# Windowed attention over two layers: position bias and mask move from eight TensorE passes per strip to eight VectorE additions

## The chip, the core and the metric

The kernel runs on one core of a Trainium2 chip. The metric is the device time of one execution in microseconds. The core has TensorE (PE in the rows: matrix passes, whose weight loads are listed apart as PEld), VectorE (DVE), ScalarE (ACT) and GpSimd (POOL), each with an instruction queue of its own, and SyncE (SP), whose queue issues all transfers here. Matrix results go into one of eight banks of PSUM; the other tiles lie in SBUF. Engines wait for each other by semaphores that count finished work.

## The reference

Two Swin layers run one after the other on `x` of 32 x 56 x 56 x 96, layer 0 with 4 heads and layer 1 with 12. In outline, for one layer:

```
h    = roll(LN(x), -3, -3), cut into windows of 7 x 7 = 49 tokens
q, k, v = h @ qkv_w + qkv_b
attn = (q * scale) @ k.T + rel_bias[head] + mask[window]      # 49 x 49, float32
o    = softmax(attn) @ v @ proj_w + proj_b
x    = x + roll(unwindow(o), 3, 3)
x    = x + fc2( [LN3, layer 0 only] gelu(LN(x) @ fc1_w + fc1_b) )
```

`rel_bias` depends on head, query and key. `mask` is 0 or -100 and differs from 0 only in the last row and the last column of windows. The term `rel_bias + mask` is what the change is about.

## The kernel before

The work is cut into 256 strips (`ns`), each a row of eight windows of one image. The eight windows lie as `PAIRS` = 4 pairs, so a strip is 4 x 98 = 392 tokens and most tiles are some 98 to 128 partitions by 392 columns. The scores of a strip stand in units of 113 x 392: the first window of each pair on partitions 0 to 48, the second on 64 to 112, and 8 blocks of 49 keys beside each other. Layer 0 has two units (`sc00`, `sc01`), layer 1 six (`sc10` to `sc15`); each has a PSUM bank while it lives.

All engines run the same loop over `i` (`iterate`), and in body `i` they work on strips of different age: `Strip(i, 2)`, called `s2`, is the strip that was loaded two bodies before. `LAST` is the largest age, so there are 256 + `LAST` bodies; those at the start and the end leave out the stages whose strip doesn't exist. The order within a body is written out by hand for each engine in its own `body(i)`. `BANKS` lists the uses of the seven shared banks (use, age, bank) in the order of TensorE's body, and `bank_free` makes a matrix pass wait until the use before it in that bank was read. The eighth bank, `ps_o`, holds the attention output.

The stages of a strip for one layer, by helper:

- `stats` (DVE), `inverse_root` and `norm` (POOL), `xT` (PE) and `turned` (ACT) normalise and transpose the tokens: tile `xnA` ahead of attention, `xnM` ahead of the MLP.
- `q`, `k`, `v` (PE) with `q_out`, `k_out`, `v_out` (ACT). `variants` and `spread_v` (SP) then rearrange keys and values by DMA into `kM` and `vM`.
- `scores` (PE). For each unit one pass `tleft` x `table` (L462, 104 rows, 113 x 392 out, start=True) writes bias and mask into the bank. Then the products of queries and keys (L471, start=False) are added to it: 24 instructions in the rows for three units of layer 1, 32 for both of layer 0.
- `shift` (DVE). The maximum over the keys, negated, is read from the bank (L826), then scores plus `negmax` go to `shifted` in SBUF (L830). That frees the bank.
- `exps` (ACT, L662), `probs_turn` (PE, L483, transpose into a `T` bank), `probsT_out` (ACT, L669), `attend` (PE, L503, into `ps_o`), `normalise` (DVE), `o_turn` (PE), `o_out` (ACT), `project` (PE), `residual` (DVE).
- `fc1` (PE, L539 to L542: three passes, of which the last needs `low_part`, a DVE subtraction, L817), `gelu` (ACT), `fc2` (PE, L559 and L565), and to finish: for layer 0 `squares` (POOL), `third_stats`, `finish0`; for layer 1 `finish1` (DVE, L861), which writes `y_out`.

Ahead of the loop the constants are loaded (L303), and DVE splits the table into a high and a low part (L786, L787).

Of the kernel before, what the change touches and what calls it, by code (L numbers as in the profile page):

```python
# [26 lines left out]
NREG = 6  # L27
BK = 2 * TOK + NREG
# [14 lines left out]
def shape_constants():  # L43
# [3 lines left out]

    left = np.zeros((BK, SP), np.float32)
    for part in (0, 1):
        for h in HALF:  # L50
            left[part * TOK + np.arange(TOK), h + np.arange(TOK)] = 1
    for q in range(TOK):
        left[2 * TOK + rr[q], HALF[0] + q] = 1
        left[2 * TOK + 2 + 2 * rr[q] + rc[q], HALF[1] + q] = 1
    k["tleft"] = left


    right = []
# [36 lines left out]
def swin_program(nc, d, out, ns=NSTRIP, last_row_from=NSTRIP - NSTRIP // ROWS_IN_IMAGE):  # L95
# [3 lines left out]
    with ctx:  # L99
# [13 lines left out]
        def rows_of(ap, step, n, *dims):  # L113
# [4 lines left out]
        tleft_in = sb("tleft_in", [BK, SP])  # L118
        tlow = sb("tlow", [BK, 1])
# [61 lines left out]
        t_in = [t[0:BK, :, :].rearrange("p u k -> p (u k)") for t in (shifted, probs)]  # L181
# [29 lines left out]
        s_s = pairsem("s_s")  # L211
        s_mx = pairsem("s_mx")
# [18 lines left out]
        BANKS = [("o1", 3, 7), ("T01", 1, 2), ("f1_1_1", 4, 5), ("xtA0", 0, 0), ("o0", 1, 7), ("oT1", 3, 1),  # L231
# [839 lines left out]
```

## Time and profile before

| | |
|---|---|
| median of 3 runs | 7130.31 us (7128.76 to 7131.41) |
| the profiled execution | 7130.83 us, its span 7129.1 us, mean granted TensorE clock 0.997 |
| instructions in the span | 284978 |
| HBM | 17 GB/s over the span; the DMA engines are 17.5% busy |

The profiled execution is within 0.6 us of the median; 1.7 us of it lie outside the span. The busy digits of all engines stay level from the second to the last but one of the 40 slices, so nearly the whole time is one repeated strip, and the fill and the drain of the pipeline are small. A busy share counts an instruction from its start to its end. TensorE and VectorE instructions overlap at their ends, so the distance from one start to the next is what one of them costs in a row of its kind.

### The profile page before, as it was taken

Reading aid. Unit: us, or ns where it says so; the run is one execution under the profiler, and the core shown is the slowest. Engines: PE = TensorE matmul, PEld = TensorE weight load, DVE = VectorE, ACT = ScalarE, POOL = GpSimd, SP = SyncE. Lnnn points to the kernel's source line nnn. Section 1 sums busy time; section 2 is a strip of 40 time slices with the busy share of each in tenths; the row PEclk is TensorE's granted clock in tenths of the full one; section 3 lists DMA queues with packets and bytes.
Section 4 is the critical chain, followed back from the end, with each engine's and each line's share of the span. In section 5 each row is a group of like instructions: output and inputs, shape, how many; then the busy total and the mean of one; then the engine's idle time right before and its main releaser. Section 6 shows DMA issues by size and latency. Waiting matters only on the chain.

```text
span 7129.1 us, 284978 instructions
## 1 busy us (share of the span) xinstructions
PE 6951.3 (98%) x98848; PEld 5895.1 (83%) x98848; DVE 5031.9 (71%) x18727; ACT 4674.0 (66%) x9220; POOL 4523.6 (63%) x4612
## 2 busy tenths in 40 slices
PE   6999999999999999999999999999999999999999
PEld 5888888888888888888888888888888888888887
DVE  5777777777777777777777777777777777777775
ACT  3666666666666666666666666666666666666665
POOL 3666666666666666666666666666666666666665
PEclk9999999999999999999999999999999999999999
DMA  1111111111111111111111111111111111111111
GB/s 49 47 46 46 46 46 45 46 45 46 45 46 45 46 45 46 45 47 45 47 45 47 45 47 45 47 44 47 44 48 44 48 44 48 43 48 43 48 43 37
DMA packets 604563, 325.43 MB, mean 46 GB/s; under 512 B 450142, under 2 KB 604128, under 8 KB 604320
## 3 DMA queue, kind: packets, MB, share of 16 engines
q1 hardware_dynamic: 604528, 324.96, 17.5%
q8 instruction: 22, 0.36, 0.0%
q14 instruction: 13, 0.11, 0.0%
HBM read 80.71 MB, written 38.54 MB: 17 GB/s over the span
## 4 chain that ended last, share of the span: by engine, by line
POOL 30%; PE 27%; issue 24%; DVE 17%; POOLq 1%; DVEq 0%; SPq 0%; DMA 0%; ACT 0%
POOL hid_sq L956 8%; POOL x_biased L947 7%; PE ps L422 5%; PE ps L526 5%; PE ps L430 5%; POOL hid_ss L958 4%; POOL rstd L967 4%; POOL rstdM L928 4%; PE ps_o L503 3%; PE ps L515 3%; POOL rstdA L928 3%; DVE x_next L890 3%; DVE bnA L801 2%; DVE bnM L801 2%; DVE o_norm L841 2%
## 5 line engine op out<-in xcount | busy, mean ns | idle before, releaser
L928 POOL TENSOR_TENSOR rstdM<-var_epsM,minus_half 98x4 f32<-98x4 f32 x512 | 515.4, 1007 | 1292.6 <-DVE var_epsM L809 1292.6
L830 DVE TENSOR_TENSOR shifted<-ps,negmax 113x392 f32<-113x392 f32 x2048 | 1161.4, 567 | 213.2
L669 ACT ACTIVATE probsT<-ps 98x392 f32<-98x392 f32 x2048 | 952.3, 491 | 431.3 <-PE ps L483 419.7
L928 POOL TENSOR_TENSOR rstdA<-var_epsA,minus_half 98x4 f32<-98x4 f32 x512 | 518.0, 1012 | 1100.0 <-DVE var_epsA L809 1100.0
L826 DVE TENSOR_REDUCE negmax<-ps 113x8 f32<-113x392 f32 x2048 | 1142.7, 558 | 56.4 <-PE ps L471 28.1
L686 ACT ACTIVATE hid<-ps,bfc 128x392 f32<-128x392 f32 x1536 | 873.0, 587 | 416.3 <-PE ps L542 399.2
L662 ACT ACTIVATE probs<-shifted 113x392 f32<-113x392 f32 x2048 | 997.7, 526 | 23.5 <-DVE shifted L830 15.2
L483 PE MATMUL ps<-ident,probs 113*98 113x113 f32 x8192 | 990.7, 264 | 9.2 <-ACT probs L662 7.7
L503 PEld LDWEIGHTS ps_o<-vM,probsT 98*49 98x49 f32 x32768 | 793.8, 125 | 195.6 <-DVE o_norm L841 128.2
L503 PE MATMUL ps_o<-vM,probsT 98*49 98x50 f32 (+1 forms) x32768 | 851.4, 201 | 78.9 <-DVE o_norm L841 78.7
L483 PEld LDWEIGHTS ps<-ident,probs 113*98 113x98 f32 x8192 | 800.9, 129 | 52.8 <-ACT probs L662 9.6
L653 ACT ACTIVATE vA<-ps 98x400 f32<-98x400 f32 (+1 forms) x512 | 260.5, 509 | 754.9 <-PE ps L440 754.9
L471 PE MATMUL ps<-kM,qT 48*49 48x98 f32 (+1 forms) x20480 | 687.2, 299 | 0.0
L559 PE MATMUL ps<-wfc,hid 128*98 128x97 f32 x6144 | 662.8, 254 | 0.0
L539 PE MATMUL ps<-xnT_high,wfc_high 96*128 96x392 f32 x1536 | 613.8, 400 | 1.2 <-ACT xnT_high L632 1.2
L559 PEld LDWEIGHTS ps<-wfc,hid 128*98 128x98 f32 x6144 | 596.7, 167 | 0.2
L956 POOL TENSOR_TENSOR hid_sq<-hid 128x1176 f32<-128x1176 f32 x256 | 549.7, 2147 | 59.8 <-ACT hid L686 59.8
L471 PEld LDWEIGHTS ps<-kM,qT 48*49 48x49 f32 (+1 forms) x20480 | 430.4, 118 | 188.4 <-issue 172.4
L559 PE MATMUL ps<-par,hid 128*98 128x96 f32 x6144 | 577.9, 251 | 0.7 <-ACT hid L686 0.7
L852 DVE TENSOR_TENSOR x_mid<-x_again,ps 98x384 f32<-98x384 f32 x256 | 141.8, 554 | 605.6 <-PE ps L526 605.6
L677 ACT ACTIVATE oT<-ps 96x392 f32<-96x392 f32 x512 | 252.4, 493 | 472.5 <-PE ps L515 472.5
L559 PEld LDWEIGHTS ps<-par,hid 128*98 128x98 f32 x6144 | 556.7, 168 | 1.2 <-ACT hid L686 1.2
(99 smaller groups left out, 15077.7 us busy)
## 6 DMA issues: line engine op xcount, KB each, us to landing
kM<-kT SPq DMA_DIRECT2D x512, 85.8 KB
vM<-vA SPq DMA_DIRECT2D x1024, 41.3 KB
vM<-vA SPq DMA_DIRECT2D x1024, 38.3 KB
x_in<-in_x SPq DMA_DIRECT2D x256, 147.0 KB
x_again<-in_x SPq DMA_DIRECT2D x256, 147.0 KB
kM<-kT SPq DMA_DIRECT2D x1024, 36.8 KB
x_keep<-x_next SPq DMA_DIRECT2D x256, 147.0 KB
out_y<-y_out SPq DMA_DIRECT2D x256, 147.0 KB
```

Of the source, the lines that this page charges most:

```text
L471: mm = pe.matmul(ps[bank_of[f"sc{L}{u}"]][HALF[h]:HALF[h] + TOK, n * p:n * (p + 1)], qT[L][r, t:t + TOK], kM[L][r, :, t:t + TOK], start=Fa ...
L483: mm = pe.transpose(ps[bank_of[f"T{L}{u}"]][0:PT, n * SP:(n + 1) * SP], probs[:, unit_buffer(L, u), n * PT:(n + 1) * PT], ident[0:SP, 0:SP])
L503: mm = pe.matmul(ps_o[HALF[h]:HALF[h] + TOK, col:col + width], probsT[:, unit_buffer(L, u), p * heads // 2 + n, h, :], vM[L][:, 2 * (first ...
L539: pe.matmul(g[:, 0:ST], wfc1_high[L][:, w], xnT_high[L][:, :], start=True, stop=False)
L559: mm = pe.matmul(g[0:PT, p * step:p * step + width], hid[L][:, c, t], w, start=(c == 0), stop=(c == HCH - 1))
L662: act.activation(probs[:, buf, :], shifted[:, buf, :], ACT.Exp).then_inc(s_ex[L], 1)
L669: act.activation(probsT[:, unit_buffer(L, u), :, :, :], free(ps[bank_of[f"T{L}{u}"]][0:PT, 0:1], (SP, 4), (64, 2), (1, TOK)), ACT.Copy).th ...
L686: act.activation(hid[L][:, c, :], ps[bank_of[f"f1_{c}_{L}"]][:, 0:ST], ACT.Gelu, bias=bfc1[L][:, c:c + 1])\
L826: dve.tensor_reduce(negmax[:, buf, :], s, AX.X, ALU.max, negate=True).then_inc(s_mx[L], 1)
L830: dve.tensor_tensor(shifted[:, buf, :].rearrange("p (h k) -> p h k", k=TOK), s, free(negmax[:, buf, 0:1], (1, 8), (0, TOK)), ALU.add).then ...
L928: pool.tensor_tensor(rstd[n][:, :], var_eps[n][:, :], minus_half[:, :], ALU.pow).then_inc(s_rstd[n], 1)
L956: pool.tensor_tensor(hid_sq[:, :, :], hid[0][:, :, :], hid[0][:, :, :], ALU.mult).then_inc(s_sq, 1)
```

## The change

The table passes L462 go. The first product of queries and keys in each piece of a bank now has start=True and overwrites it. A new helper `bias` on DVE adds the table to the bank in place, 113 x 392 in float32, and counts `s_sb`, for which `shift` now waits; `shift` itself is as before. The table is kept as float32 on 113 partitions (mask loaded from a host array, then two additions ahead of the loop) instead of as a split pair on 104. DVE also clears seven banks ahead of the loop. `scores` waits for queries, keys and banks first and then issues its products. For layer 0 there is one new pass of 1 x 1 ahead of them.

The written-out orders of all five queues are new, as are the banks, and `LAST` is 5 instead of 4: attention of layer 0 is now finished at age 1 and 2, layer 1 starts at age 3.

```diff
-LAST = 4
+LAST = 5
@@ constants
-        t_high = sb("t_high", [BK, NT], f32r)
-        tleft = sb("tleft", [BK, SP], f32r)
-        table = sb("table", [BK, 2 * NT], f32r)
+        table = sb("table", [SP, 2 * NT])
@@ loads
-        loads = [(ident[:, :], d["ident"]), (tleft_in[:, :], d["tleft"]), (tlow[:, :], d["tlow"])]
-        for v in (0, 1):
-            loads += [(t_in[v][0:2 * TOK, :], d["tab"]), (t_in[v][2 * TOK:BK, :], d["tmask"][:, v * NT:(v + 1) * NT])]
+        loads = [(ident[:, :], d["ident"]), (t_in, d["tab"]), (table[:, :], d["mask"])]
@@ scores
-                for u in units:
-                    if free_from := bank_free(x, f"sc{L}{u}"):
-                        pe.wait_ge(*free_from)
-                    if u == units[-1]:
-                        pe.wait_ge(s_qe[L], x.count(1, 1))
-                        pe.wait_ge(s_km[L], x.count(16 * VARIANTS[L], 16 * VARIANTS[L]))
-                    pe.matmul(ps[bank_of[f"sc{L}{u}"]][0:SP, 0:UNIT_COLS], tleft[:, :], table_of(x, L, u),
-                              start=True, stop=False, skip_group_check=True)
+                pe.wait_ge(s_qe[L], x.count(1, 1))
+                pe.wait_ge(s_km[L], x.count(16 * VARIANTS[L], 16 * VARIANTS[L]))
+                for free_from in banks_free(x, [f"sc{L}{u}" for u in units]):
+                    pe.wait_ge(*free_from)
+                if L == 0:
+
+                    pe.matmul(ps[bank_of["sc00"]][0:1, 0:1], ident[:, 0:1], ident[:, 0:1], start=True, stop=True, skip_group_check=True)
...
-                                           kM[L][r, :, t:t + TOK], start=False, stop=True, skip_group_check=True)
+                                           kM[L][r, :, t:t + TOK], start=True, stop=True, skip_group_check=True)
@@ DVE, ahead of the loop
+            for bank in ps[:7]:
+                dve.memset(bank[:, :], 0.0).then_inc(s_memset, 1)
...
-            dve.tensor_copy(tleft[:, :], tleft_in[:, :])
             for v in (0, 1):
                 half = slice(v * NT, (v + 1) * NT)
-                done(dve.tensor_copy(t_high[:, :], t_in[v]))
-                done(dve.scalar_tensor_tensor(out=table[:, half], in0=t_high[:, :].bitcast(f32), scalar=tlow[:, 0:1],
-                                              in1=t_in[v], op0=ALU.mult, op1=ALU.add))
+                done(dve.tensor_tensor(table[:, half], table[:, half], t_in, ALU.add))
@@ DVE, in the loop
+            def bias(x, L, u):
+
+                if x.exists(ns):
+                    dve.wait_ge(s_s[L], x.count(UNITS[L], u + 1))
+                    s = ps[bank_of[f"sc{L}{u}"]][0:SP, 0:UNIT_COLS]
+                    dve.tensor_tensor(s, s, table_of(x, L, u), ALU.add).then_inc(s_sb[L], 1)
+
             def shift(x, L, u):
                 if not x.exists(ns):
                     return
-                dve.wait_ge(s_s[L], x.count(UNITS[L], u + 1))
+                dve.wait_ge(s_sb[L], x.count(UNITS[L], u + 1))
@@ TensorE's body: the first lines, and the last
+                o_turn(s2, 0)
+                xT(s3, "A1")
+                o_turn(s4, 1)
+                project(s2, 0)
+                k(s3, 1)
+                fc1(s5, 1, 0)
+                project(s4, 1)
...
+                xT(s2, "M0")
+                scores(s3, 1, (0, 1, 2))
...
                 attend(s1, 0, 0)
                 attend(s1, 0, 1)
+                scores(s0, 0, (0, 1))
+                xT(s4, "M1")
```

How TensorE's queue moves. Before, from the transpose of `xnM` (layer 0, age 1) to the first `fc1` of layer 0:

```order
L414 MATMUL ps<-ident,xnM 96x98 x4
L462 ISA
L462 MATMUL ps<-table,tleft 113x392
L462 ISA
L462 MATMUL ps<-table,tleft 113x392
L461 REGISTER_ALU
L462 ISA
L462 MATMUL ps<-table,tleft 113x392
L471 MATMUL ps<-kM,qT 49x196 x12
L539 MATMUL ps<-xnT_high,wfc_high 128x392
```

The same place now, from `xnM` of layer 0 (age 2) on, the line numbers being those of the changed kernel (L459 scores, L471 turn of probabilities, L527 fc1):

```order
L411 MATMUL ps<-ident,xnM 96x98 x4
L446 ISA
L459 MATMUL ps<-kM,qT 49x196 x12
L469 REGISTER_ALU
L471 MATMUL ps<-ident,probs 98x113 x4
L527 MATMUL ps<-xnT_high,wfc_high 128x392
```

The three table passes are gone, and a turn of probabilities of layer 0 stands between the scores and `fc1`.

TensorE's later queue now, between the second turn of layer 1's probabilities and the end of its attention:

```order
L471 MATMUL ps<-ident,probs 98x113 x4
L469 REGISTER_ALU
L471 MATMUL ps<-ident,probs 98x113 x4
L491 MATMUL ps_o<-vM,probsT 49x18 x24
L469 REGISTER_ALU
L471 MATMUL ps<-ident,probs 98x113 x8
L467 REGISTER_ALU
L471 MATMUL ps<-ident,probs 98x113 x4
L491 MATMUL ps_o<-vM,probsT 49x18 x24
```

Before, all six `attend` calls of layer 1 (48 rows of 49x18) stood together at the top of the body. Now they are in two halves, in the body in which the scores were made.

VectorE's queue before, from `low_part` of layer 0 into the shifts of layer 1:

```order
L817 TENSOR_TENSOR xnT_low<-ps,xnT_high 96x392
L823 REGISTER_ALU
L826 TENSOR_REDUCE negmax<-ps 113x8
L828 REGISTER_ALU
L830 TENSOR_TENSOR shifted<-ps,negmax 113x392
L823 REGISTER_ALU
L826 TENSOR_REDUCE negmax<-ps 113x8
L828 REGISTER_ALU
L830 TENSOR_TENSOR shifted<-ps,negmax 113x392
```

The same place now (L812 low_part, L820 bias, L828 and L832 shift):

```order
L812 TENSOR_TENSOR xnT_low<-ps,xnT_high 96x392
L818 ISA
L820 ISA
L820 TENSOR_TENSOR ps<-ps,table 113x392
L818 REGISTER_ALU
L820 ISA
L820 TENSOR_TENSOR ps<-ps,table 113x392
L818 REGISTER_ALU
L820 ISA
L820 TENSOR_TENSOR ps<-ps,table 113x392
L828 TENSOR_REDUCE negmax<-ps 113x8
```

Three additions now stand between `low_part` and the first shift. Behind the three shifts come `finish1`, two more additions, two shifts, one addition, `third_stats` and the last shift.

## Rows read from the trace of the kernel before

**Rows 1.** The page, busy time of each engine (share of span):
```profile
PE 6951.3 (98%) x98848; PEld 5895.1 (83%) x98848; DVE 5031.9 (71%) x18727; ACT 4674.0 (66%) x9220; POOL 4523.6 (63%) x4612
```

**Rows 2.** Groups by line, TensorE and ScalarE: busy us, mean ns, idle before:
```profile
L503 PE MATMUL ps_o<-vM,probsT 98*49 98x50 f32 (+1 forms) x32768 | 851.4, 201 | 78.9 <-DVE o_norm L841 78.7
L462 PE MATMUL ps<-table,tleft 104*113 (+1 forms) x2048 | 531.5, 361 | 4.0 <-DMA kM<-kT 2.2 <-DVE shifted L830 1.3 <-DVE y_out L861 0.5
L662 ACT ACTIVATE probs<-shifted 113x392 f32<-113x392 f32 x2048 | 997.7, 526 | 23.5 <-DVE shifted L830 15.2
```

**Rows 3.** Timeline, VectorE, y_out of strips 2 and 252 (start us, us):
```profile
186.21 0.55 DVE L861 TENSOR_TENSOR y_out<-x_biased,ps 98x384 f32<-98x384 f32 x1
...
7036.04 0.55 DVE L861 TENSOR_TENSOR y_out<-x_biased,ps 98x384 f32<-98x384 f32 x1 [0.21 <-PE ps L559]
```

**Rows 4.** Timeline, TensorE, second half of one steady strip:
```profile
3526.72 2.24 PE L559 MATMUL ps<-par,hid 128*98 128x96 f32 x24
3528.80 0.86 PE L440 MATMUL ps<-wqkv,xnT 97*98 97x100 f32 x8
3529.49 0.50 PE L414 MATMUL ps<-ident,xnM 98*96 98x98 f32 x4
3529.78 0.77 PE L462 MATMUL ps<-table,tleft 104*113 x3
3530.48 0.89 PE L471 MATMUL ps<-kM,qT 32*49 32x196 f32 x24
3531.30 0.45 PE L539 MATMUL ps<-xnT_high,wfc_high 96*128 96x392 f32 x1
...
3533.01 0.70 PE L462 MATMUL ps<-table,tleft 104*113 x3
...
3535.22 0.59 PE L462 MATMUL ps<-table,tleft 104*113 x2
3535.74 0.89 PE L471 MATMUL ps<-kM,qT 48*49 48x98 f32 x32
```

**Rows 5.** Timeline, TensorE, fc2, probability turns and attend of the strip before:
```profile
3511.09 1.20 PE L559 MATMUL ps<-wfc,hid 128*98 128x97 f32 x12
...
3513.80 1.34 PE L483 MATMUL ps<-ident,probs 113*98 113x113 f32 x12
3514.92 0.42 PE L539 MATMUL ps<-xnT_high,wfc_high 96*128 96x392 f32 x1
...
3515.62 2.38 PE L503 MATMUL ps_o<-vM,probsT 98*49 98x18 f32 x96
```

**Rows 6.** Timeline, ScalarE: copy of the xnM turn:
```profile
3530.11 0.49 ACT L632 ACTIVATE xnT_high<-ps 96x392 fp32r<-96x392 f32 x1
```

**Rows 7.** Timeline, VectorE: shifts, third statistics, low part:
```profile
3504.69 0.57 DVE L830 TENSOR_TENSOR shifted<-ps,negmax 113x392 f32<-113x392 f32 x1
3505.18 0.56 DVE L826 TENSOR_REDUCE negmax<-ps 113x8 f32<-113x392 f32 x1
3505.84 0.57 DVE L830 TENSOR_TENSOR shifted<-ps,negmax 113x392 f32<-113x392 f32 x1
...
3513.98 0.17 DVE L869 COPY st<-ps 98x8 f32<-98x8 f32 x1
...
3514.75 0.56 DVE L826 TENSOR_REDUCE negmax<-ps 113x8 f32<-113x392 f32 x1
...
3530.73 0.56 DVE L817 TENSOR_TENSOR xnT_low<-ps,xnT_high 96x392 fp32r<-96x392 f32 x1 [1.09 <-ACT xnT_high L632]
```

**Rows 8.** Timeline, start of the kernel:
```profile
22.77 1.24 PE L385 MATMUL ps<-par 96*1 96x324 f32 x2 [22.77 <-DMA wproj<-in_wproj]
...
35.15 1.79 DVE L786 CAST t_high<-shifted 104x3136 fp32r<-104x3136 f32 x1
...
45.84 0.74 DVE L801 BATCH_NORM_STATS2 bnA<-x_in 98x6 f32<-98x96 f32 x4
```

**Rows 9.** DMA issues: out<-in, queue, op, count, KB each:
```profile
shifted<-in_tab SPq DMA_DIRECT2D x1, 1200.5 KB
```

More of the change, by code:

```diff
@@ L26 @@
 EPS = 1e-5
-NREG = 6
-BK = 2 * TOK + NREG
 UNIT_COLS = 8 * TOK
@@ L45, in shape_constants @@
     k = {"ident": np.eye(128, dtype=np.float32)}
[L48 to L58, printed above, removed]
+    masks = []
     for last_row in (0, 1):
@@ L179, in swin_program @@
         rstd3 = sb("rstd3", [PT, PAIRS])
-        t_in = [t[0:BK, :, :].rearrange("p u k -> p (u k)") for t in (shifted, probs)]
+        t_in = shifted[:, :, :].rearrange("p u k -> p (u k)")
         ps = [psum_bank(f"ps{n}") for n in range(7)] + [psum_bank("ps_o")]
@@ L269, in bank_free, with banks_free @@
                 if bank == bank_of[use] and y.exists(ns):
-                    semaphore, per, c = over[other]
-                    return semaphore, y.count(per, c)
-            return None
+                    return y, over[other]
+            return None
+        def bank_free(x, use):
+            if found := released(x, use):
+                y, (semaphore, per, c) = found
+                return semaphore, y.count(per, c)
+            return None
+        def banks_free(x, uses):
+            last = {}
+            for found in [released(x, use) for use in uses]:
+                if found:
+                    y, (semaphore, per, c) = found
+                    name = semaphore.name
+                    if name not in last or c - y.off * per > last[name][0]:
+                        last[name] = c - y.off * per, semaphore, y.count(per, c)
+            return [(semaphore, count) for _, semaphore, count in last.values()]
         def unit_buffer(L, u):
             return u + L * UNITS[0]
-        loads = [(ident[:, :], d["ident"]), (tleft_in[:, :], d["tleft"]), (tlow[:, :], d["tlow"])]
-        for v in (0, 1):
-            loads += [(t_in[v][0:2 * TOK, :], d["tab"]), (t_in[v][2 * TOK:BK, :], d["tmask"][:, v * NT:(v + 1) * NT])]
+        loads = [(ident[:, :], d["ident"]), (t_in, d["tab"]), (table[:, :], d["mask"])]
         for L in (0, 1):
@@ L895, in body @@
             def body(i):
-                s0, s1, s2, s3, s4 = Strip(i, 0), Strip(i, 1), Strip(i, 2), Strip(i, 3), Strip(i, 4)
+                s0, s1, s2, s3, s4, s5 = Strip(i, 0), Strip(i, 1), Strip(i, 2), Strip(i, 3), Strip(i, 4), Strip(i, 5)
                 stats(s0, "A0")
+                normalise(s2, 0)
+                bias(s1, 0, 0)
+                shift(s1, 0, 0)
+                low_part(s5, 1)
+                residual(s2, 0)
+                stats(s2, "M0")
+                bias(s1, 0, 1)
+                shift(s1, 0, 1)
+                residual(s4, 1)
+                stats(s4, "M1")
+                low_part(s2, 0)
+                bias(s3, 1, 0)
+                bias(s3, 1, 1)
+                bias(s3, 1, 2)
+                shift(s3, 1, 0)
+                shift(s3, 1, 1)
+                shift(s3, 1, 2)
+                finish1(s5)
+                bias(s3, 1, 3)
+                bias(s3, 1, 4)
+                shift(s3, 1, 3)
+                shift(s3, 1, 4)
+                bias(s3, 1, 5)
                 third_stats(s2)
-                shift(s1, 0, 1)
+                shift(s3, 1, 5)
                 finish0(s2)
```

205 lines of the change are left out of this document (88 added, 117 removed), and 12 rows, old and new, of the table BANKS.

## Prediction

> **What bounds the kernel now.** I first read the busy shares on the page [rows 1]: TensorE 98%, VectorE 71%, ScalarE 66%, GpSimd 63%. A share alone could mislead, since the ends of matrix passes are modelled, so next came the groups by line [rows 2]. In the loop TensorE's one idle spell of any size is 78.9 us ahead of `attend`, for `o_norm`: 78.9 / 256 = 0.31 us per strip. TensorE issues practically without a gap, and the other engines wait for it. Then the timeline. The starts of `y_out` give the period P of a strip [rows 3]: (7036.04 - 186.21) / 250 = 27.40 us. What lies outside these 250 periods is 7129.1 - 6849.8 = 279.3 us. So time = 279.3 + 250 x P + 1.7 us outside the span. It is the sum against the profiled execution, 7130.8 us, which stands 0.5 us above the median of the runs.
>
> **Removed: the table passes.** There are 8 per strip (2048 in all, [rows 2]). Their price is read from start to start, not from the 361 ns of one, because passes overlap. Three passes take 29.78 to 30.48 = 0.70 us, two take 35.22 to 35.74 = 0.52 us [rows 4]. Hence a pass is 0.18, and 0.16 is the switch from full-height passes to the small ones of the scores. That switch stays, since now a turn, `fc2` or the 1 x 1 pass stands ahead. I take off 8 x 0.18 = 1.44 us; 1.85, all three stretches whole, is the upper end.
>
> **Added on TensorE.** The order splits layer 1's `attend` in halves, so there is one switch more: 0.16 in, and about 0.1 out, 0.25 together. The 1 x 1 pass of layer 0 is shown by no row. It costs between nothing and 0.18 + 0.16 (a pass and a switch); I take 0.10, as it has one column and the queue waits for nothing new there. `o_norm` no longer holds TensorE, since `scores(s0, 0)` and `xT(s4, "M1")` now stand between `attend(s1, 0, 1)` and `o_turn`: 0.31 goes. TensorE's work is then 27.40 - 0.31 - 1.44 + 0.25 + 0.10 = 26.0 us per strip.
>
> **Added on VectorE.** Eight additions of 113 x 392 in float32 from a bank and SBUF into the bank. No row shows an addition whose output is a bank. The nearest is `shifted`, same shape, float32, bank to SBUF: 0.57 us long, and the next instruction starts 3505.18 - 3504.69 = 0.49 later [rows 7]. When the next one needs its result, as the addition of a maximum does, the step is 3505.84 - 3505.18 = 0.66. So an addition costs 0.49 to 0.66; I take 0.49, because in the order six of eight are followed by something that doesn't read their result. Two (both of layer 0) are followed by their own maximum and cost 0.66. The sum is 6 x 0.49 + 2 x 0.66 = 4.3 us of VectorE per strip. Its load of 5031.9 / 256 = 19.7 us [rows 1] becomes 19.7 + 8 x 0.57 = 24.2, 91% of the period that I forecast. VectorE isn't full, but it has little room left, so where its work stands decides.
>
> The page *VectorE: DVE Perf Modes* of the Trainium skill says, in "The DRAIN you can't avoid", that the next Vector op does not start until the pipe has emptied. The rows disagree for independent ops: the maximum starts 0.08 us before the addition ahead of it ends. Were the rule right for an op that writes a bank, the step would be at least 0.57.
>
> **The stretch that decides.** It begins with `xT(s2, "M0")` on TensorE and ends when TensorE can turn the last unit of layer 1, `probs_turn(s3, 1, 5)`. Two chains run beside each other.
>
> TensorE's work in it, from starts in [rows 4] and [rows 5]: `xT` 0.29; scores of layer 1 twice 0.82; a turn of one unit 1.12 / 3 = 0.37, five of them before the last, and one of layer 0, 2.24; `fc1` three times 1.71; `fc2` of layer 1 2.08; `k` 0.7 (an estimate, four times a pass of 0.18); `fc2` of layer 0 3513.80 - 3511.09 = 2.71; half of the attention 2.38 / 2 = 1.19; two switches 0.32. Sum 12.9 us.
>
> VectorE's chain: from `xT` over ScalarE's copy to `low_part` 3530.73 - 3529.49 = 1.24 [rows 4, 6, 7]; `low_part` about 0.49; six additions 2.94; five whole shifts 0.49 + 0.66 = 1.15 each, 5.75; the sixth until its end 0.66 + 0.57 = 1.23; `finish1` about 0.49; `third_stats` 3514.75 - 3513.98 = 0.77 [rows 7]. Sum 12.9. Then `exps` 0.53 [rows 2] and two handovers of about 0.1: 13.6 us.
>
> The second chain is longer by 13.6 - 12.9, rounded up to 0.75 from the unrounded sums, and TensorE has to wait that long before `probs_turn(s3, 1, 5)`. In the kernel before nothing like it exists, since `attend` of layer 1 came a body later. So P = 26.0 + 0.75 = 26.75 us.
>
> **Moved, costed at nothing.** The added wait for `s_s` holds VectorE at `bias(s1, 0, 0)`; behind it stand `low_part(s5, 1)` and `residual(s2, 0)`, for which GpSimd and then `xT(s2, "M0")` wait. TensorE has twelve calls between `o_turn(s2, 0)` and `xT(s2, "M0")`, and these hide it; without that cover each microsecond counts fully. On SP, `spread_v` of layer 1 now stands ahead of that of layer 0, and `variants(s0, 0)` near the end. Values are needed at `attend`, keys of layer 0 at the last but one call of the body; the calls between hide both. `squares` on GpSimd has to be done in the middle of `fc2(s2, 0)`; TensorE would wait there, but inside the stretch in which it waits anyway. The waits of `shift` for `s_sb` are within VectorE.
>
> **Ends.** `LAST` = 5 adds one partial body; the drain shows its size: (7129.1 - 7036.0) / 4 = 23.3 us. Constants: the tables were 2 x 1200.5 KB [rows 9] and are now 113 x 3136 and 113 x 6272 floats, 4153 KB. All 3556 KB of constants had landed after 22.8 us [rows 8], some 160 KB per us, so 1560 KB more are 10 us (15 if only the tables' 2401 KB count in the rate, nothing if the transfers run wider on 113 rows). The split took 45.84 - 35.15 = 10.7 us [rows 8], of which the two casts are 3.6. Two additions of the same length as what is left are 7.1, so 3.6 are saved. The cleared banks lie under the load. Ends: 279.3 + 23.3 + 6 = 308.6 us.
>
> **Sum.** 308.6 + 250 x 26.75 + 1.7 = 6998; I forecast 7000 us. Break-even with the execution before is P = (7129.1 - 308.6) / 250 = 27.28.
>
> **Rivals.**
>
> 1. *TensorE stays the only bound.* VectorE's chain is no longer than TensorE's, because the handovers are shorter or more of a switch is lost on TensorE. P = 26.0 or a little less, time 6810. For it: the queues were laid out anew. Against it: the sums above differ by 0.75, and VectorE is at 91%.
> 2. *Each addition is charged in full.* The step is 0.57, its length, as in the skill's rule above. Worked out from the rows: 6 x 0.08 = 0.5 us more on the chain, P = 27.25, time 7123: no change that can be told. For it: no row has a bank as output. Against it: every row of VectorE with float32 and a bank as input starts its successor early.
> 3. *VectorE becomes the bound, slower.* The write back into the same bank must have ended before the next instruction starts, as between dependent ones: 0.66 or 0.67 per addition, place the six additions of layer 1, price 6 x 0.18 = 1.1 us. P = 27.85, time 7273. It decides from a step of 0.49 + (27.28 - 26.75) / 6 = 0.58 us on. The register work for the table's address, which moves from TensorE's queue to VectorE's, could add to it. Against it: that register work runs while the instruction ahead is busy.
> 4. *The change doesn't save what it removes,* since the passes were hidden. TensorE is 98% busy and nothing runs over them; the rows give no chance of its own to this.
>
> **How the numbers follow.** Forecast 0.62, with its own range 6840 to 7075 (P from 26.15 to 27.0: 1.85 in place of 1.44 one way, the 1 x 1 pass at 0.34 the other, 0.1 per handover, ends by 10 us). Rival 1 0.15, rival 2 0.10, rival 3 0.13. The range 6830 to 7130 leaves out most of rival 1 and rival 3, a little over 0.2. Within 0.2% means 7116 to 7144.5, about what a measurement of this kernel can tell from no change. It gets half of rival 2, 0.05; its other half falls below. Faster: 0.62 + 0.15 + 0.05 = 0.82. Slower: rival 3, 0.13.
>
> **What would show it.** In the profile after: no table pass; period of `y_out` 26.75; TensorE about 97% busy with an idle spell of some 0.7 us per strip ahead of a turn of probabilities, released by `probs`; an addition of 0.57 us with its successor 0.49 later; VectorE near 91%; first TensorE pass near 33 us. I am wrong if the step of an addition is 0.58 or more (rival 3), if TensorE has no idle spell (rival 1), or if the wait stands at `xT(s2, "M0")`, `o_turn` or the scores instead, which would say that a cover costed at nothing is gone.

## The result, and the profile after

| | before | changed |
|---|---|---|
| median | 7130.31 us (7128.76 to 7131.48, 5 runs) | 7165.39 us (7164.81 to 7166.33, 5 runs) |
| ratio | | 1.0049, 95% interval 1.0035 to 1.0064 |
| span of the profiled execution | 7129.1 us | 7163.6 us |
| period of `y_out` | 27.40 us | 26.93 us |
| start of the first TensorE pass | 22.77 us | 169.02 us |

The change makes the kernel 0.5% slower, where 7000 us were forecast. The strip became shorter, nearly as forecast. The start became 146 us longer, which was not forecast at all.

The page of the changed kernel, busy time per engine, and of its slices the rows of TensorE, of the DMA engines' busy share and of GB/s. They answer to [rows 1].

```profile
PE 6826.1 (95%) x97312; PEld 5745.8 (80%) x97312; DVE 6149.6 (86%) x20779; ACT 4743.2 (66%) x9220; POOL 4522.6 (63%) x4612
...
PE   0799999999999999999999999999999999999999
...
DMA  0111111111111111111111111111111111111111
GB/s 30 37 48 45 48 46 46 48 46 46 48 44 47 48 44 47 49 44 47 48 44 48 47 45 48 46 46 48 45 47 48 44 47 48 44 47 49 44 47 35
```

TensorE's first slice, 179 us wide, is empty while 30 GB/s move. TensorE's 95% would be read wrongly without this row: it is idle in the first slice and not in the loop.

The start of the changed kernel: the first row of TensorE, the first statistics on VectorE with the table's additions ahead of them [rows 8], and the long rows of the queue that issues the transfers.

```profile
169.02 1.24 PE L382 MATMUL ps<-par 96*1 96x324 f32 x2 [169.02 <-DMA wproj<-in_wproj]
```

```profile
181.28 6.88 DVE L775 TENSOR_TENSOR table<-table,shifted 113x3136 f32<-113x3136 f32 x2
188.19 0.74 DVE L796 BATCH_NORM_STATS2 bnA<-x_in 98x6 f32<-98x96 f32 x4
```

```profile
1.58 20.57 SPq L300 DMA_DIRECT2D table<-in_mask  x1
22.19 80.58 SPq L300 DMA_DIRECT2D par<-in_par  x2
```

The same two `par` loads in the kernel before:

```profile
3.53 0.82 SPq L303 DMA_DIRECT2D par<-in_par  x2
```

The queue is held up behind its own transfers: issuing these two loads took 0.82 us, and takes 80.58 here. A stretch of the start, in the changed kernel (start and end, length, busy us and count of PE, PEld, DVE, ACT and POOL, granted clock, DMA share, GB/s):

```profile
30.00:100.00 70.00, 0.00 (x0) 0.00 (x0) 0.00 (x0) 0.00 (x0) 0.00 (x0) 1.00 0.08 30
```

The 16 DMA engines together are 8% busy, hardly more than the 6% that a single busy one would make.

The loop in the changed kernel, VectorE's `y_out` of strips 2 and 251, which answer to [rows 3]. (7048.54 - 342.15) / 249 = 26.93 us.

```profile
342.15 0.54 DVE L863 TENSOR_TENSOR y_out<-x_biased,ps 98x384 f32<-98x384 f32 x1
...
7048.54 0.55 DVE L863 TENSOR_TENSOR y_out<-x_biased,ps 98x384 f32<-98x384 f32 x1
```

VectorE between `low_part` and the last shift of a steady strip (L820 is the addition, L828 the maximum, L832 the addition of `negmax`, L875 part of `third_stats`). It answers to [rows 7].

```profile
3515.59 1.51 DVE L820 TENSOR_TENSOR ps<-ps,table 113x392 f32<-113x392 f32 x3
3517.01 0.55 DVE L828 TENSOR_REDUCE negmax<-ps 113x8 f32<-113x392 f32 x1
...
3524.79 0.40 DVE L875 SCALAR_TENSOR_TENSOR var<-st 98x4 f32<-98x4 f32 x1
...
3526.16 0.57 DVE L832 TENSOR_TENSOR shifted<-ps,negmax 113x392 f32<-113x392 f32 x1
```

Three additions take 1.42 us from the first start to the maximum, 0.47 each. That was the step I chose (0.49). The groups by line of VectorE in the changed kernel (mean ns before the second bar), for the lengths:

```profile
L832 DVE TENSOR_TENSOR shifted<-ps,negmax 113x392 f32<-113x392 f32 x2048 | 1160.9, 567 | 212.9
...
L820 DVE TENSOR_TENSOR ps<-ps,table 113x392 f32<-113x392 f32 x2048 | 1088.1, 565 | 5.4 <-PE ps L459 5.3
L804 DVE TENSOR_SCALAR var_epsA<-mvA 98x4 f32<-98x4 f32 x512 | 211.0, 412 | 17.6
```

TensorE in the changed kernel: the wait ahead of `o_turn` (L503), the start of the stretch that the prediction calls decisive (`xnM` of layer 0, L411), and the turns (L471) between the two halves of layer 1's attention with the weight load of the last of them.

```profile
3505.29 0.54 PE L411 MATMUL ps<-ident,xnM 98*96 98x98 f32 x4
3506.15 0.59 PE L503 MATMUL ps<-ident,o_norm 113*96 113x113 f32 x4 [0.32 <-DVE o_norm L843]
...
3513.88 0.50 PE L411 MATMUL ps<-ident,xnM 98*96 98x98 f32 x4
...
3526.43 1.52 PE L471 MATMUL ps<-ident,probs 113*98 113x113 f32 x12
3527.87 1.28 PE L491 MATMUL ps_o<-vM,probsT 98*49 98x18 f32 x48
```

```profile
3527.34 0.37 PEld L471 LDWEIGHTS ps<-ident,probs 113*98 113x98 f32 x4 [0.17 <-ACT probs L650]
```

Three units' turns take 1.44 us until the `attend` behind them starts. The 1.12 of [rows 5] is no measure for that, since no switch to small passes stood behind those three. Where nothing holds them, three turns ahead of an `attend` take 1.30 us (runs 6 and 11). So 0.14 us of waiting lies inside the row, and the weight load shows what it is for: `probs`. The bracket of 0.32 for `o_norm` is the one that I said would go.

What holds `o_norm` up, in the changed kernel: VectorE's statistics of `s0` ahead of it, and GpSimd beside them.

```profile
3502.18 0.17 DVE L804 TENSOR_SCALAR var_epsA<-mvA 98x4 f32<-98x4 f32 x1
...
3504.51 0.66 DVE L804 TENSOR_SCALAR var_epsA<-mvA 98x4 f32<-98x4 f32 x1
...
3505.46 0.56 DVE L843 TENSOR_TENSOR o_norm<-ps_o,rden 113x384 f32<-113x384 f32 x1
3505.93 0.56 DVE L820 TENSOR_TENSOR ps<-ps,table 113x392 f32<-113x392 f32 x1
3506.53 0.57 DVE L828 TENSOR_REDUCE negmax<-ps 113x8 f32<-113x392 f32 x1
```

```profile
3504.32 0.83 POOL L949 TENSOR_TENSOR xnA<-xnA,rstdA 98x384 f32<-98x384 f32 x1
...
3524.34 0.83 POOL L949 TENSOR_TENSOR xnM<-xnM,rstdM 98x384 f32<-98x384 f32 x1
```

The same instruction takes 0.17 us where GpSimd is idle, and 0.66 where it starts inside L949. It ends at 3505.17, when L949 ends (3505.15). L875 in `third_stats` ends at 3525.19, when the other L949 ends (3525.17). In both cases VectorE's instruction ends with GpSimd's.

### The profile page after: what moved, and what is told of

Read it like the earlier page. It is cut to its first block, busy times and chain, and to the rows that moved or that the text cites. A ratio compares the mean times of both kernels' runs of the same rounds, so it can differ in the third digit from the quotient of the medians.

```text
span 7163.6 us, 283376 instructions
## 1 busy us (share of the span) xinstructions
PE 6826.1 (95%) x97312; PEld 5745.8 (80%) x97312; DVE 6149.6 (86%) x20779; ACT 4743.2 (66%) x9220; POOL 4522.6 (63%) x4612
## 4 chain that ended last, share of the span: by engine, by line
DVE 33%; issue 30%; POOL 22%; PE 10%; SPq 2%; DVEq 2%; POOLq 1%; ACT 0%; DMA 0%; ACTq 0%
POOL hid_sq L966 8%; DVE bnA L796 5%; DVE bnM L796 5%; DVE x_mid L854 4%; POOL rstd L977 4%; POOL hid_ss L968 4%; PE ps L503 3%; POOL x_biased L957 3%; PE ps L514 3%; DVE x_next L892 3%; POOL xnM L945 3%; DVE mvA L801 2%; DVE mvM L801 2%; DVE rden L839 2%; SPq L300 2%
## 5 line engine op out<-in xcount | busy, mean ns | idle before, releaser
L832 DVE TENSOR_TENSOR shifted<-ps,negmax 113x392 f32<-113x392 f32 x2048 | 1160.9, 567 | 212.9
L650 ACT ACTIVATE probs<-shifted 113x392 f32<-113x392 f32 x2048 | 1025.3, 525 | 405.9 <-DVE shifted L832 372.8
L828 DVE TENSOR_REDUCE negmax<-ps 113x8 f32<-113x392 f32 x2048 | 1143.2, 558 | 17.5
L471 PE MATMUL ps<-ident,probs 113*98 113x113 f32 x8192 | 1092.1, 268 | 5.2 <-DVE shifted L832 3.2
L820 DVE TENSOR_TENSOR ps<-ps,table 113x392 f32<-113x392 f32 x2048 | 1088.1, 565 | 5.4 <-PE ps L459 5.3
L491 PEld LDWEIGHTS ps_o<-vM,probsT 98*49 98x49 f32 x32768 | 823.6, 125 | 253.6 <-ACT probsT L657 212.3
L471 PEld LDWEIGHTS ps<-ident,probs 113*98 113x98 f32 x8192 | 783.5, 130 | 214.5 <-ACT probs L650 121.9
L491 PE MATMUL ps_o<-vM,probsT 98*49 98x50 f32 (+1 forms) x32768 | 899.2, 202 | 15.9 <-DVE o_norm L843 0.7
L459 PE MATMUL ps<-kM,qT 32*49 32x196 f32 (+1 forms) x20480 | 688.6, 299 | 22.5 <-ACT hid L674 3.8
L527 PE MATMUL ps<-xnT_high,wfc_high 96*128 96x392 f32 x1536 | 650.8, 424 | 2.3 <-ACT hid L674 1.7
L620 ACT ACTIVATE xnT_high<-ps 96x392 fp32r<-96x392 f32 x512 | 252.2, 493 | 538.3 <-PE ps L411 501.4
L459 PEld LDWEIGHTS ps<-kM,qT 32*49 32x49 f32 (+1 forms) x20480 | 447.2, 118 | 107.6 <-issue 65.6
L530 PE MATMUL ps<-xnT_low,wfc_high 96*128 96x392 f32 x1536 | 526.9, 343 | 0.0
```

The lines of the kernel that those rows point to most:

```text
L459: mm = pe.matmul(ps[bank_of[f"sc{L}{u}"]][HALF[h]:HALF[h] + TOK, n * p:n * (p + 1)], qT[L][r, t:t + TOK], kM[L][r, :, t:t + TOK], start=Tr ...
L471: mm = pe.transpose(ps[bank_of[f"T{L}{u}"]][0:PT, n * SP:(n + 1) * SP], probs[:, unit_buffer(L, u), n * PT:(n + 1) * PT], ident[0:SP, 0:SP])
L491: mm = pe.matmul(ps_o[HALF[h]:HALF[h] + TOK, col:col + width], probsT[:, unit_buffer(L, u), p * heads // 2 + n, h, :], vM[L][:, 2 * (first ...
L650: act.activation(probs[:, buf, :], shifted[:, buf, :], ACT.Exp).then_inc(s_ex[L], 1)
L820: dve.tensor_tensor(s, s, table_of(x, L, u), ALU.add).then_inc(s_sb[L], 1)
L828: dve.tensor_reduce(negmax[:, buf, :], s, AX.X, ALU.max, negate=True).then_inc(s_mx[L], 1)
```

## Experiments

"Split loads" below is the changed kernel with its two table loads cut in two. It serves as the base of most runs, because its start is as short as before.

### 1. The start: rows 0 to 111 and row 112 as loads of their own

Edit on the changed kernel:

```diff
-        loads = [(ident[:, :], d["ident"]), (t_in, d["tab"]), (table[:, :], d["mask"])]
+        loads = [(ident[:, :], d["ident"])]
+        for dst, src in ((t_in, d["tab"]), (table[:, :], d["mask"])):
+            loads += [(dst[0:112, :], src[0:112, :]), (dst[112:SP, :], src[112:SP, :])]
```

> The changed kernel, with each of its two table loads issued as rows 0 to 111 and row 112. Theory R (row count): a transfer of 113 rows runs on one DMA engine (4153 KB in the 169 us before the first pass, 28 GB/s), one of 112 rows is spread. Then the first TensorE pass starts near 32 us instead of 169.0, the period of y_out stays 26.93, and the time falls by about 137 us to 7028 (ratio to before 0.986). Rival B (bytes): the load is slow because it is 1600 KB more in longer rows, or because the queue holds too few entries; then the first pass stays near 169 us and the time near 7165.

Measured: 7030.61 us (7027.45 to 7031.92), ratio 0.9858 (0.9841 to 0.9874), period 26.94. TensorE's first row with split loads:

```profile
28.27 1.24 PE L384 MATMUL ps<-par 96*1 96x324 f32 x2 [28.27 <-DMA wproj<-in_wproj]
```

In the stretch from 3 to 28 us the DMA engines are 76% busy and move 199 GB/s, against 8% and 30 GB/s in the changed kernel. The same bytes arrive 141 us earlier. This edit alone turns 0.5% slower into 1.4% faster.

### 2. The same trap laid in the kernel before

The two loads of 98 rows become 97 rows and one row:

```diff
-            loads += [(t_in[v][0:2 * TOK, :], d["tab"]), (t_in[v][2 * TOK:BK, :], d["tmask"][:, v * NT:(v + 1) * NT])]
+            loads += [(t_in[v][0:97, :], d["tab"][0:97, :]), (t_in[v][97:98, :], d["tab"][97:98, :]), (t_in[v][2 * TOK:BK, :], d["tmask"][:, v * NT:(v + 1) * NT])]
```

> The kernel before, with its two loads of the 98-row table issued as rows 0 to 96 and row 97; same bytes. Theory R: 97 rows have no divisor but 1 up to 16, so 2 x 1188 KB go at 28 GB/s, 87 us, on one or two DMA engines: first TensorE pass near 95 us instead of 22.8 (near 55 if the two transfers take different engines), time 7160 to 7205. Rival B: the bytes are the same, so first pass 23 us and time 7130.

Measured: 7217.34 us, ratio 1.0121 (1.0101 to 1.0141), period 27.40. The first pass:

```profile
103.60 1.24 PE L385 MATMUL ps<-par 96*1 96x324 f32 x2 [103.60 <-DMA wproj<-in_wproj]
```

The load is 81 us longer with nothing added but a cut. First pass and time both lie above what was expected (near 95 us, and 7205 at most). So the row count decides: 97 rows are slow and 98 fast, 113 slow and 112 fast. The slow pieces moved at about the same rate in both kernels: 2 x 97 x 3136 floats (2434 KB) in some 99 us and 4153 KB in some 164 us, 25 KB per us (estimates, with 5 us taken off for the rest). My expectations had 28 in place of these 25, which is why they came out short.

### 3. The additions taken out

Split loads, `bias` issues nothing, and `shift` waits for `s_s` again (bias and mask are left out).

```diff
-                dve.wait_ge(s_sb[L], x.count(UNITS[L], u + 1))
+                dve.wait_ge(s_s[L], x.count(UNITS[L], u + 1))
@@ bias
-                if x.exists(ns):
+                if False:
```

> As e1_rows112, with the eight additions of the table left out (position bias and mask are missing from the scores). Theory V: the chain through VectorE holds the period above TensorE's own work, so without 3.9 us of additions the period falls from 26.93 to about 26.2 (TensorE's sum was 26.0), time near 6850. Rival T: TensorE is the bound in the new order, the period stays within 0.15 of 26.93, time near 7010.

Measured: 7026.63 us (7016.73 to 7028.07), ratio 0.9854 (0.9838 to 0.9871), period 26.92 against 26.94. Eight additions, 4.25 us of VectorE per strip, cost the kernel nothing measurable. Theory V is wrong. VectorE without them, at the start of `third_stats`:

```profile
3515.84 0.17 DVE L873 COPY st<-ps 98x8 f32<-98x8 f32 x1 [1.68 <-PE ps L555]
```

VectorE is done early, and then waits 1.68 us for `fc2(s2, 0)`. The last shift stands behind `third_stats` and comes no sooner. So it is released by two chains that end nearly together, by VectorE's shifts and additions, and by TensorE's `fc2`: from the start of the last passes of `fc2` (L555 here, L553 there) to the copy it is 0.47 us here, and 0.57 in the changed kernel.

### 4. One more instruction on that chain

Split loads, and one maximum over the constant table ahead of the last addition (0.47 us to the next start):

```diff
+                    if (L, u) == (1, 5):
+                        dve.tensor_reduce(spare[:, :], table[:, 0:UNIT_COLS].rearrange("p (h k) -> p h k", k=TOK), AX.X, ALU.max)
```

> As e1_rows112, with one more VectorE maximum of 113 x 392 per strip, over the constant table, right ahead of the addition of unit 5 of layer 1; its result is not used. Theory E (the additions just fill VectorE's wait for fc2 of layer 0, and nothing is left over): third_stats starts 0.3 to 0.5 us later and the period rises by 0.3 to 0.5, time 7105 to 7160. Rival T (TensorE's order alone sets the period, VectorE has room): within 0.1, 7010 to 7055.

Measured: 7083.42 us, ratio 0.9931 (0.9915 to 0.9946), period 27.15, which is 0.21 more. The turns between the halves of the attention, now in two rows:

```profile
3494.10 0.98 PE L474 MATMUL ps<-ident,probs 113*98 113x113 f32 x8
3495.24 0.59 PE L474 MATMUL ps<-ident,probs 113*98 113x113 f32 x4 [0.16 <-ACT probs L653]
3495.77 1.28 PE L494 MATMUL ps_o<-vM,probsT 98*49 98x18 f32 x48
```

They take 1.67 us, 0.23 more than in the changed kernel. About half of the added 0.47 comes through, and all of it at the turn that I named. The other half was taken up behind the maximum, in `third_stats`:

```profile
3492.03 0.83 POOL L954 TENSOR_TENSOR xnM<-xnM,rstdM 98x384 f32<-98x384 f32 x1
```

```profile
3492.92 0.16 DVE L880 SCALAR_TENSOR_TENSOR var<-st 98x4 f32<-98x4 f32 x1
```

The square now starts after GpSimd is through (3492.86) and lasts 0.16 us, 0.163 on the mean of all strips, where it lasts 0.424 with split loads alone. The maximum delays the chain by 0.47 and removes a stall of 0.26 from it, which leaves 0.21: the chain has next to no slack, as theory E says.

### 5. The stall beside GpSimd

Split loads, and the epsilon is added by a sum over (variance, epsilon):

```diff
-        mv = {n: sb("mv" + n, [PT, PAIRS, 2]) for n in LN}
+        mv = {n: sb("mv" + n, [PT, PAIRS, 3]) for n in LN}
@@ stats; mv[:, :, 2] is set to EPS once, and two accesses to mv follow its new shape
-                dve.tensor_scalar(var_eps[n][:, :], free(mv[n][:, 0, 1:2], (2, PAIRS)), EPS, None, ALU.add)\
+                dve.tensor_reduce(var_eps[n][:, :], mv[n][:, :, 1:3], AX.X, ALU.add)\
```

> As e1_rows112 (period 26.94, 7031 us), but VectorE adds epsilon to the variance with a tensor_reduce over the pair variance, epsilon instead of a tensor_scalar. Theory S: the tensor_scalar of xnA, which lasts 0.66 instead of 0.17 while GpSimd works, makes o_norm late and TensorE wait 0.3 us ahead of o_turn; if the reduce does not stall (0.17 us), the wait goes and the period falls by 0.2 to 0.3, time 6955 to 6980. Rival L: another wait takes its place (the last turn of layer 1's probabilities), the period stays within 0.1, time 7005 to 7031.

Measured: 6916.89 us (6914.58 to 6921.34), ratio 0.9695 (0.9682 to 0.9708), period 26.50. That is 0.44 us per strip, more than the 0.3 that I expected. The edit changes all four of these sums in a strip, but only one of them was held up: of `var_epsA` every second one (0.17 and 0.66 us, 412 ns on the mean), of `var_epsM` none (170 ns). The groups of VectorE with this edit, and TensorE at `o_turn`, where the bracket is gone:

```profile
L879 DVE SCALAR_TENSOR_TENSOR var<-st 98x4 f32<-98x4 f32 x256 | 109.9, 429 | 8.8
L808 DVE TENSOR_REDUCE var_epsA<-mvA 98x4 f32<-98x8 f32 x512 | 82.9, 162 | 17.6
```

```profile
3502.92 0.54 PE L413 MATMUL ps<-ident,xnM 98*96 98x98 f32 x4
3503.31 0.59 PE L505 MATMUL ps<-ident,o_norm 113*96 113x113 f32 x4
```

From the turn of `xnM` to `o_turn` it is 0.39 us from start to start, and 0.86 in the changed kernel. This difference of 0.47 covers the whole gain. The bracket of 0.32 had shown only part of the wait.

### 6. The second stall of the same kind

As run 5, and in `third_stats` one operand of the square comes from the bank:

```diff
-                dve.scalar_tensor_tensor(out=var3[:, :], in0=st3[:, :, 0], scalar=-1.0, in1=st3[:, :, 0],
+                dve.scalar_tensor_tensor(out=var3[:, :], in0=free(g[0:PT, C:C + 1], (C + 2, PAIRS)), scalar=-1.0, in1=st3[:, :, 0],
```

> The version with split loads and the epsilon by a sum, and in third_stats the square of the mean takes one of its operands from the bank instead of from SBUF. That instruction lasts 0.43 us there instead of 0.16, and it stands ahead of the last maximum. Theory S (two SBUF operands on VectorE are what GpSimd holds up, and the time lost ahead of the last shift is lost for TensorE): it lasts 0.16 to 0.2, period 26.3 to 26.4, 6865 to 6895 us. Rival T (time there is covered): the instruction may be shorter, period stays 26.5, 6910 to 6922 us. Rival G (where the operand comes from doesn't matter): it still lasts 0.43.

Measured: 6877.27 us (6875.21 to 6879.86), ratio 0.9642 (0.9629 to 0.9655), period 26.34. This is the fastest version found. Its groups:

```profile
L882 DVE TENSOR_TENSOR var<-var,st 98x4 f32<-98x4 f32 x256 | 57.5, 225 | 8.8
...
L879 DVE SCALAR_TENSOR_TENSOR var<-ps,st 98x4 f32<-98x4 f32 x256 | 41.4, 162 | 8.9
```

The square takes 162 ns instead of 429. The next instruction, both of whose operands are in SBUF, takes up a little of the stall (225 instead of 162). The turns between the halves take 1.30 us instead of 1.44, as many as where nothing holds them (two turns ahead of an `attend` take 0.90, one more is 0.37): the wait is gone, and the period falls by about as much. Rivals T and G are wrong.

### 7. The additions once more, with the first stall gone

As run 5 without the additions (bias and mask are left out, the edit is that of run 3).

> The version with split loads and the epsilon by a sum, without the eight additions (bias and mask are left out). Period with them 26.50. Theory T (TensorE's queue sets the period and VectorE's eight additions are hidden, as they were at 26.94): 26.45 to 26.50, 6905 to 6920 us. Rival V (with the stall gone VectorE's chain from low_part to the last shift is what is left ahead of the last turn, 0.32 us of wait): the wait goes, period 26.2 and 6840 us or less.

Measured: 6918.23 us, ratio 0.9699 (0.9685 to 0.9712), period 26.53. The additions still cost nothing. Runs 6 and 7 fit together if the last turn hangs on `fc2(s2, 0)`, `third_stats` and the last shift: a shorter `third_stats` brings it forward, and taking the additions away doesn't.

### 8. Is the sum simply the better instruction?

The edit of run 5 in the kernel before.

> The kernel before, with the epsilon added by a sum over (variance, epsilon) in place of a tensor_scalar. Theory S (the gain in the changed kernel came from a VectorE tensor_scalar that is held up while GpSimd works): in the kernel before this instruction lasts 0.17 us and isn't held up, so nothing is gained here, 7120 to 7140 us, period 27.40. Rival (a sum is simply the cheaper way everywhere, stall or not): the gain carries over, 7030 us or less, period 27.0.

Measured: 7142.78 us, ratio 1.0014 (1.0005 to 1.0023). Nothing is gained, so the gain of run 5 was the stall alone. In the kernel before, this instruction lasts 170 ns throughout (median of `var_epsA` and of `var_epsM`, and at most 172).

### 9. The removal alone, in the kernel before

The table passes are taken out of the kernel before, the 1 x 1 pass is put in, and nothing takes their place (bias and mask are left out). The products get start=True and the banks are cleared, as in the changed kernel.

```diff
-                    pe.matmul(ps[bank_of[f"sc{L}{u}"]][0:SP, 0:UNIT_COLS], tleft[:, :], table_of(x, L, u),
-                              start=True, stop=False, skip_group_check=True)
```

> The kernel before with its eight table passes left out and the 1 x 1 pass added (position bias and mask are missing from the scores), old order, LAST = 4. Theory P (passes are paid in full): the period falls from 27.40 by 1.4 to 1.85 less 0.1 for the 1 x 1 pass, to 25.6 to 26.1, time 6690 to 6820. Rival H: other waits fill the gap, as in the changed kernel, period above 26.5 and time above 6910.

Measured: 7090.82 us, ratio 0.9939 (0.9924 to 0.9955), period 27.24. Of the 1.34 us that TensorE no longer issues (1.44 less the 1 x 1 pass), 0.16 reach the time. TensorE in this run:

```profile
3495.52 0.99 PE L483 MATMUL ps<-ident,probs 113*98 113x113 f32 x8 [0.35 <-ACT vA L653]
...
3502.45 2.38 PE L503 MATMUL ps_o<-vM,probsT 98*49 98x18 f32 x96 [0.24 <-DMA vM<-vA]
...
3506.57 0.94 PE L503 MATMUL ps_o<-vM,probsT 98*49 98x50 f32 x32 [0.32 <-DVE o_norm L843]
```

The first two brackets, 0.59 us together, are new: the passes had covered a copy of ScalarE and a DMA. The third, for `o_norm`, was there before (0.31). The rest of the 1.18 us that did not reach the time lies in shorter waits that carry no bracket on TensorE; one of them is for `low_part` (0.30 us ahead of the weight load of L542, in nearly every strip). Rival 4 of my prediction, to which the rows "give no chance of its own", is right for the old order.

### 10. The additions in the old order

Split loads, with the orders, the banks and `LAST` of the kernel before, each addition right ahead of its own shift.

> As e1_rows112 (additions on VectorE, table passes gone), but with the orders, banks and LAST = 4 of the kernel before; each addition stands right ahead of its shift. Theory V: every addition then costs 0.66 in VectorE's queue, layer 1's part 4 us ahead of the last probabilities, so the period is 27.4 or more and the time 7100 to 7250. Rival O: VectorE was idle 6.3 us per strip for others in the old order and swallows the additions, period about 26.3 and time near 6850; the new order would not be needed.

Measured: 8422.12 us, ratio 1.1808 (1.1788 to 1.1828), period 32.43, mean granted clock 0.919. TensorE:

```profile
3491.32 0.60 PE L473 MATMUL ps<-ident,probs 113*98 113x113 f32 x4 [1.79 <-DVE shifted L834]
...
3493.07 1.71 PE L473 MATMUL ps<-ident,probs 113*98 113x113 f32 x8 [0.81 <-DVE shifted L834]
```

The direction was right and the size far off. In the old order the additions cost 32.43 - 27.24 = 5.2 us per strip (against run 9), some of it by the lower clock; in the new one they cost nothing (run 3). Without them the two orders differ by only 27.24 - 26.92 = 0.3 us. So the new order is what makes the additions free. Which part of it does that, the order of the queues, the banks or the extra age, was not tried.

### 11. The last shift ahead of `third_stats`

Split loads, two lines of VectorE's body exchanged:

```diff
-                third_stats(s2)
                 shift(s3, 1, 5)
+                third_stats(s2)
```

> As e1_rows112, with the last shift of layer 1 ahead of third_stats in VectorE's queue instead of behind it. Theory F (the chain fc2 of layer 0, third_stats, last shift, exp, last turn holds TensorE for 0.3 us): the last exp comes about 1 us earlier, that wait goes, the period falls by 0.2 to 0.3, time 6955 to 6980. Rival D: third_stats and with it GpSimd's root and finish0 come 0.5 to 1.1 us later, VectorE reaches normalise later, and the wait at o_turn grows by as much: period up by 0.2 to 0.8, time 7080 to 7230.

Measured: 7615.58 us, ratio 1.0675 (1.066 to 1.0689), mean period 29.25, mean granted clock 0.930. The last turn does come earlier (the three units take 1.30 us instead of 1.44), but VectorE now waits 1.29 us for GpSimd's `rstd`, and TensorE for VectorE's `o_norm`:

```profile
3517.20 1.58 PE L493 MATMUL ps_o<-vM,probsT 98*49 98x50 f32 x32 [1.21 <-DVE o_norm L845]
...
3518.83 1.56 PE L461 MATMUL ps<-kM,qT 48*49 48x98 f32 x32
```

Rival D is right. Behind the idle spell TensorE's passes take nearly twice as long (1.56 for the 0.89 of [rows 4]). Two stretches of this run, in the form of the one above, show why:

```profile
3517.20:3522.00 4.80, 4.80 (x76) 4.42 (x77) 3.61 (x15) 0.49 (x1) 4.26 (x6) 0.50 0.00 0
3522.00:3527.00 5.00, 5.00 (x38) 4.66 (x37) 3.31 (x14) 3.58 (x7) 0.37 (x1) 0.81 0.00 0
```

The granted clock is 0.98 from 3515.00 to 3517.20, where TensorE is busy for 0.99 of 2.20 us, then 0.50, the level of 1.2 GHz, until some time behind 3522, and 1.00 again, the level of 2.4 GHz, from 3527 to 3532. One strip later the same wait (1.18 us) is followed by passes of the usual length:

```profile
3547.40 0.94 PE L493 MATMUL ps_o<-vM,probsT 98*49 98x50 f32 x32 [1.18 <-DVE o_norm L845]
...
3548.39 0.89 PE L461 MATMUL ps<-kM,qT 48*49 48x98 f32 x32
```

## Why the prediction was wrong

**The step that failed is "Ends", its line on the constants.** I put +10 us of load for 1560 KB more, with bounds from 0 to 15, at the rate of the kernel before. The load took 146.25 us more (169.02 - 22.77). The rate was carried over to transfers of another shape: the tables' 98 rows became 113. I had even written the row count down, as a reason for a faster load ("if the transfers run wider on 113 rows"). Runs 1 and 2 show that the count decides, in either kernel, and in the other direction. The Trainium skill states it (*DMA: Bandwidth & Descriptors*, "Why a DMA increments its semaphore by 16 and not by 1"): a DMA is divided among the largest number of engines, at most 16, that divides the slowest dimension of both access patterns. By that rule 112 rows get 16 engines, 98 get 14, and the primes 97 and 113 get one. The runs agree in all four cases, 112 and 98 rows being fast, 113 and 97 slow. So does the DMA engines' busy share: 0.08 from 30 to 100 us of the changed kernel, where one busy engine of 16 would make 0.06, and 0.76 with split loads.

The remainder of that term: VectorE's setup became 23.07 - 19.17 = 3.9 us shorter, as predicted (3.6). The fill from the first statistics to the `y_out` of strip 2 became 13.6 us longer and the drain about 4 shorter, together +9.6 where one partial body of 23.3 was predicted.

The whole account against 7163.6 - 6996.1 (span forecast) = 167.5: constants +136.3 (142.3 measured, 6 predicted), fill and drain -13.7, and 250 x (26.93 - 26.75) = +45.

**The period was 0.18 us off, from errors of which one, the last turn, cancels most of the others.**

- TensorE's work: 26.0 predicted. Measured as the period less the waits seen, 26.93 - 0.47 (`o_norm`) - 0.14 (last turn) - 0.28 - 0.15 (both below) = 25.9. Right within 0.1. The 1 x 1 pass starts its successor 0.12 us later (0.10 predicted).
- The wait at `probs_turn(s3, 1, 5)`: place right, size 0.14 instead of 0.75. VectorE's chain came out nearly as summed: from `xT` (3513.88) to the weight load of the last turn (3527.34) it is 13.5 us, and 13.6 were predicted. TensorE's side was summed too short: it could have begun the last turn 2 x 0.37 us after 3526.43, so its own share is 13.3 and not 12.9. Beyond that, run 3 shows that the last shift is held nearly as much by `fc2(s2, 0)` through `third_stats`, a chain that I had left out, so taking away the additions, 2.9 us of my chain, shortens nothing.
- `o_norm` no longer holding TensorE: wrong. The calls that I named do lie between, but `o_norm` comes later too, because `var_epsA` of `s0` in front of it is held up for 0.5 us by GpSimd. The bracket of 0.31 stayed as 0.32, and by run 5 the whole wait is 0.47.
- Not foreseen, two waits for banks. Which bank it is was read from `BANKS` in the changed kernel, and no run takes either wait away. The scores of layer 1 start 0.57 us after `xT(s2, "M0")` instead of 0.29: `sc10` shares bank 4 with the turn of `xnA`, which ScalarE copies until 3514.35. The two passes of `q(s3, 1)` (from 3510.81) take 0.81 us until `fc1(s5, 1, 1)` instead of the 0.66 that two such passes take from 3520.74 on: this `fc1` shares bank 6 with the `fc1` before it, which ScalarE's `hid` reads until 3511.57.

```profile
3511.62 0.19 PEld L527 LDWEIGHTS ps<-xnT_high,wfc_high 96*128 96x128 f32 x1 [0.64 <-ACT hid L674]
```

The sum of the errors is -0.1 + 0.47 + 0.28 + 0.15 - 0.61 = 0.19 against 26.93 - 26.75 = 0.18.

Rival 1 (TensorE the only bound, P = 26.0) is refuted for this kernel by these waits. With the two stalls taken out the period is still 26.34 (run 6).

Rivals 2 and 3 (an addition charged at 0.57 or 0.66) are refuted: 0.47 to the next independent instruction, 0.60 to the dependent one. The form that writes its own bank costs what `shifted` costs, 565 against 567 ns. Where I set a rule of the Trainium skill beside the rows (*VectorE: DVE Perf Modes*, "The DRAIN you can't avoid"), I had quoted half of it: the section adds that a next instruction that isn't held starts earlier. The rows agree with that half: between independent additions the step of 0.47 us is about 0.1 shorter than the instruction.

The stalls do follow a page of the Trainium skill (*SBUF — State Buffer*, "Who interferes with whom"). VectorE and GpSimd share a pair of SBUF ports. An instruction of VectorE that uses the pair, such as a `tensor_scalar` in a two-port mode, blocks until GpSimd is through if GpSimd issued first. One with two SBUF operands contends with a GpSimd instruction that reads SBUF, and `tensor_reduce` never contends on this chip. Whether the `tensor_scalar` here ran in a two-port mode no row shows. The lengths agree: `tensor_scalar` 0.66 against 0.17, the square with two SBUF operands 429 ns and with one 162, `tensor_reduce` 162 in the same place.

**Rival 4** got no chance, and run 9 shows that it holds in the old order: a TensorE that is 98% busy need not be 98% necessary. In the new order, too, most of the saving was eaten by waits: the period fell by 0.47 us. That it fell at all needed the new order, by which the additions cost nothing (runs 3 and 10).

## What to carry to other kernels

Price a transfer by its shape and not by its bytes alone: before a tile gets another number of rows, factor it, and read the start in the trace of the kernel before for what rate each shape had. Removing work from an engine that is never idle shortens the time only by the distance to the next late arrival, so ask for each stretch that is shortened which result arrives next (run 9 kept 0.16 of 1.34 us). A wait can be longer than its bracket, or have none: compare the distance between starts with a run in which nothing holds them. A new order brings instructions of VectorE and GpSimd together that had never met; a tiny instruction of two and a half to four times its usual length ahead of a critical one is worth looking for, and here the two of them were worth 2.2% (7030.6 to 6877.3 us).

## What the runs showed of the hardware

- A load of 113 or 97 rows moved at some 25 KB per us, one of 112 or 98 rows many times faster: with 112 rows and one row apart, all 5116 KB of constants had landed after 28.3 us (run 1).
- A VectorE addition with two float32 operands, bank and SBUF, that writes into the bank it reads takes 565 ns for 113 x 392, and its independent successor starts 0.47 us after it, its dependent one 0.60.
- Beside a GpSimd instruction of 98 x 384 (0.83 us), a VectorE `tensor_scalar` of 98 x 4 lasted 0.66 us in the strip shown instead of 0.17, and a `scalar_tensor_tensor` of 98 x 4 with both operands in SBUF 0.43 on the mean instead of 0.16. A `tensor_reduce` in place of the first, and a bank operand in the second, lasted 0.16 (runs 5 and 6).
- TensorE's clock fell to half in some steady strips of runs 10 and 11, behind idle spells of 1.2 us and more; the mean was 0.92 and 0.93. In the changed kernel the longest idle spell in the steady rows shown is 0.32 us, and the mean was 0.995. In run 11 one such fall cost about 2.3 us: from `attend` (3517.20) to `project` it took 5.96 us, in the strip behind it 4.03 with a wait of 0.35 in it. Two strips with about the same spell differed in this, so a spell of this length alone doesn't decide it, and what else does wasn't tried.
